# Graph network on one core: pair sums of the GAT passes made by TensorE and copied by ScalarE

## The reference

```python
def gatv2(x, src, dst, Wl, bl, Wr, br, att, bias, heads, out_ch):
    xl = (x @ Wl + bl).reshape(n, heads, out_ch)
    xr = (x @ Wr + br).reshape(n, heads, out_ch)
    e = jax.nn.leaky_relu(xl[src] + xr[dst], 0.2)
    score = jnp.einsum('ehc,hc->eh', e, att)
    smax = jax.ops.segment_max(score, dst, num_segments=n)
    ex = jnp.exp(score - smax[dst])
    denom = jax.ops.segment_sum(ex, dst, num_segments=n)
    alpha = ex / (denom[dst] + 1e-16)
    out = jax.ops.segment_sum(xl[src] * alpha[:, :, None], dst, num_segments=n)
```

## Time and profile before

| | |
|---|---|
| median of three runs | 7723.91 us |
| profiled execution, its own time | 7727.08 us |
| its span, first to last instruction | 7725.4 us |
| mean granted TensorE clock | 0.73 |
| busy: VectorE, GpSimd | 5362.1 us (69%), 4934.9 us (64%) |
| busy: TensorE products, weight loads | 4529.9 us (59%), 4074.4 us (53%) |
| busy: ScalarE | 870.3 us (11%) |
| first GAT pass, first gather to the pass's last add | 2569 to 3721 us |
| second GAT pass, likewise | 3782 to 4928 us |

### The profile page before, as it was taken

The page is one execution under the profiler, slowest core; times in us unless marked ns, Lnnn a source line. Parts: engine busy times, 40 slices in busy tenths (PEclk is TensorE's granted clock), DMA queues, the critical chain, the costliest instruction groups (busy, mean ns, idle before and its releaser), DMA issues. The chain is left out here.

```text
span 7725.4 us, 86513 instructions
## 1 busy us (share of the span) xinstructions
PE 4529.9 (59%) x24887; PEld 4074.4 (53%) x24887; DVE 5362.1 (69%) x14083; ACT 870.3 (11%) x2697; POOL 4934.9 (64%) x5168
## 2 busy tenths in 40 slices
PE   0444444566663466666466666675666677666665
PEld 0444343555553455555355555665555567555554
DVE  4333334577777799999799999647777744777776
ACT  0333332000000000000000000110000012000001
POOL 0777774777773577777377777227777702777771
PEclk8666666677776677777677777787777778777777
DMA  1444443666663344444344444456666635666662
GB/s 49 154 161 151 161 154 79 213 211 216 205 215 96 110 149 150 149 149 149 89 148 149 148 149 149 119 196 214 209 217 208 209 102 190 216 208 217 212 212 68
DMA packets 396869, 1264.58 MB, mean 164 GB/s; under 512 B 121860, under 2 KB 175678, under 8 KB 310014
## 3 DMA queue, kind: packets, MB, share of 16 engines
q1 hardware_dynamic: 195086, 766.00, 27.1%
q0 software_dynamic: 201328, 493.18, 22.5%
HBM read 1085.24 MB, written 173.47 MB: 163 GB/s over the span
## 5 line engine op out<-in xcount | busy, mean ns | idle before, releaser
L686 POOL DMA_INDIRECT gathered_rows<-table_l,gather_index x4176 | 4091.7, 980 | 1878.9 <-issue 1240.8
L1197 PE MATMUL ps<-weighted_rows,onehot 128*128 128x136 f32 (+2 forms) x8320 | 1744.9, 380 | 1508.4 <-DVE acc L1054 1507.1
L1197 PEld LDWEIGHTS ps<-weighted_rows,onehot 128*128 128x128 f32 x8320 | 1541.2, 274 | 1673.1 <-DVE acc L1054 914.7
L1164 PE MATMUL ps<-dst_side,onehot_t 128*128 x8320 | 1591.6, 353 | 140.3 <-issue 96.2
L1164 PEld LDWEIGHTS ps<-dst_side,onehot_t 128*128 128x128 f32 x8320 | 1456.3, 263 | 169.8 <-issue 98.7
L1054 DVE TENSOR_TENSOR acc<-acc,ps 128x136 f32 (+2 forms) x4160 | 1186.6, 285 | 108.6 <-PE ps L1197 7.6
L957 DVE TENSOR_TENSOR products<-gathered_rows,ps 128x512 f32<-128x512 f32 x836 | 565.1, 676 | 520.9 <-issue 227.9
L768 DVE TENSOR_TENSOR acc<-acc,ps 128x128 f32 x832 | 238.8, 287 | 693.7 <-PE ps L805 671.6
L977 DVE TENSOR_REDUCE scores<-products 128x16 f32<-128x512 f32 (+2 forms) x1040 | 709.4, 682 | 13.3
L686 POOL DMA_INDIRECT weights<-table_l,gather_index x612 | 579.6, 947 | 186.5 <-issue 172.8
L805 PE MATMUL ps<-gathered_rows,onehot 128*128 128x128 f32 x1664 | 351.5, 377 | 568.5 <-ACT gathered_rows L744 567.3
(11 more groups left out here) (283 smaller groups left out, 4450.9 us busy)
## 6 DMA issues: line engine op xcount, KB each, us to landing
onehot_t<-onehots_turned SPq DMA_DIRECT2D x260, 1024.0 KB
onehot<-onehots SPq DMA_DIRECT2D x260, 1024.0 KB, 5.2
gathered_rows<-table_l,gather_index POOLq DMA_INDIRECT x4176, 2.5
onehots<-onehot SPq DMA_DIRECT2D x52, 1024.0 KB, 6.9
onehots_turned<-onehot_t SPq DMA_DIRECT2D x52, 1024.0 KB, 4.2
table_l<-gathered_rows SPq DMA_DIRECT2D x50, 1024.0 KB, 4.4
segment_flags_sb<-segment_flags SPq DMA_DIRECT2D x1300, 8.2 KB
onehot<-type_mask_rows SPq DMA_DIRECT2D x50, 256.0 KB, 5.2
```

The lines of the kernel that those rows point to most:

```text
L686: pool.indirect_dma_start(out=home(v, t // GC)[:, t % GC, :], out_offset=None, in_=table, in_offset=bass.IndirectOffsetOnAxis(ap=e.idx[:, ...
L1164: ins = nc.tensor.matmul(ps[:, BZ + k, g * P:(g + 1) * P], e.ohT[:, u, t * P:(t + 1) * P], kRows[:, bass.ds(bs[t % 8], D)], start=True, st ...
L1197: ins = nc.tensor.matmul(ps[:, BP + n % 4, 256 * g:256 * g + PW], e.oh[:, u, t, :], exvT[:, t, :], start=True, stop=True)
```

## The change

In a GAT pass `dst_rows` on TensorE first multiplies the identity with the chunk's gathered rows, 512 columns in one product, and then accumulates the four destination products on it, so that the PSUM bank holds the pair sums. For that TensorE waits for the gathered rows. ScalarE copies the bank to `prod` (`keep_pair_sums`). VectorE's `product` is now the leaky step itself: the maximum of 0.2 times the bank and of the copy; `leaky` is gone. TensorE may write the bank again once that step is done, and ScalarE may write `prod` again once the score of two chunks earlier is done. Passes without `gat` are as before.

```diff
--- before.py
+++ after.py
@@ -907,6 +907,15 @@
                 e.oht_here[u].wait(act, a_no, 16 * (q + 1))
                 nc.scalar.activation(e.col0[:, u:u + 1], e.ohT[:, u, 0:1], ACT.Copy).then_inc(e.column_kept.sem, 1)
 
+            def keep_pair_sums(s, j):
+                if gat:
+                    c, k = J * s + j, j % 2
+                    e.z_ready.wait(act, a_no, c + 1)
+                    if not (static(s, 1) and j < 2):
+
+                        e.score_ready.wait(act, a_no, c - 1)
+                    nc.scalar.activation(e.prod[:, k, :], ps[:, BZ + k, :], ACT.Copy).then_inc(e.zc_ready.sem, 1)
+
             def keep_scores(s):
                 e.turned_ready.wait(act, a_no, s + 1)
                 if not static(s, 1):
@@ -933,11 +942,18 @@
                 if chain:
                     keep_scores(s - 1)
                 if cur:
+                    keep_pair_sums(s, 1)
                     keep_column(s, u, q)
+                    keep_pair_sums(s, 2)
                 if chain:
                     open_scale(s - 1, 1 - u)
                     exps(s - 1)
-
+                if cur:
+                    keep_pair_sums(s, 3)
+                    if ahead:
+                        keep_pair_sums(s + 1, 0)
+
+            keep_pair_sums(0, 0)
             for s in range(ways):
                 slot(s, s, 0, chain=s > 0, weigh=s > 1)
             turns(slot, ways, NG - 1, ways)
@@ -949,23 +965,22 @@
         def _(dve):
             def product(s, w, qw, j):
                 c, k = J * s + j, j % 2
+                if gat:
+                    e.zc_ready.wait(dve, gat_no, c + 1)
+                    V.scalar_tensor_tensor(e.prod[:, k, :], ps[:, BZ + k, :], 0.2, e.prod[:, k, :], ALU.mult, ALU.max)\
+                        .then_inc(e.prod_ready.sem, 1)
+                    return
                 v, qv = buffer(w, qw)
                 e.z_ready.wait(dve, a_no, c + 1)
                 here[v][j].wait(dve, here_no, 64 * (qv + 1))
                 if not (static(s, 1) and j < 2):
                     e.score_ready.wait(dve, a_no, c - 1)
                 V.tensor_tensor(e.prod[:, k, :].rearrange("p (g d) -> p g d", d=D), home(v, j)[:, :, 0:D],
-                                ps[:, BZ + k, :].rearrange("p (g d) -> p g d", d=D), ALU.add if gat else ALU.mult).then_inc(e.prod_ready.sem, 1)
-
-            def leaky(s, j):
+                                ps[:, BZ + k, :].rearrange("p (g d) -> p g d", d=D), ALU.mult).then_inc(e.prod_ready.sem, 1)
+
+            def weight_att(s, j):
                 if gat:
                     e.prod_ready.wait(dve, a_no, J * s + j + 1)
-                    pr = e.prod[:, j % 2, :]
-                    V.scalar_tensor_tensor(pr, pr, 0.2, pr, ALU.mult, ALU.max).then_inc(e.leaky_step.sem, 1)
-
-            def weight_att(s, j):
-                if gat:
-                    e.leaky_step.wait(dve, gat_no, J * s + j + 1)
                     pr = e.prod[:, j % 2, :].rearrange("p (g d) -> p g d", d=D)
                     V.tensor_tensor(pr, pr, att.unsqueeze(1).to_broadcast([P, GC, D]), ALU.mult).then_inc(e.att_step.sem, 1)
 
@@ -1093,8 +1108,6 @@
                     product(s, w, qw, 0)
                 if chain:
                     chain_backward(r, v)
-                if cur:
-                    leaky(s, 0)
                 if chain:
                     hand_back_ends(r)
                 if cur:
@@ -1111,8 +1124,6 @@
                 if weighs:
                     add(p, 3, bp[3])
                 if cur:
-                    leaky(s, 1)
-                if cur:
                     weight_att(s, 1)
                     score(s, 1)
                 if chain:
@@ -1126,7 +1137,6 @@
                 if weighs:
                     add(p, 5, bp[5])
                 if cur:
-                    leaky(s, 2)
                     weight_att(s, 2)
                 if weighs:
                     add(p, 6, bp[6])
@@ -1136,7 +1146,6 @@
                     add(p, 7, bp[7])
                 if cur:
                     product(s, w, qw, 3)
-                    leaky(s, 3)
                     weight_att(s, 3)
                     score(s, 3)
 
@@ -1155,14 +1164,20 @@
         def _(pe):
             def dst_rows(s, w, qw, j, bs):
                 u, q = two(w, qw)
+                v, qv = buffer(w, qw)
                 c, k = J * s + j, j % 2
+                if gat:
+                    here[v][j].wait(pe, here_no, 64 * (qv + 1))
                 if not (static(s, 1) and j < 2):
 
                     e.prod_ready.wait(pe, a_no, c - 1)
+                if gat:
+
+                    nc.tensor.matmul(ps[:, BZ + k, :], e.ident[:, :], home(v, j).rearrange("p g d -> p (g d)"), start=True, stop=False)
                 for g in range(GC):
                     t = GC * j + g
                     ins = nc.tensor.matmul(ps[:, BZ + k, g * P:(g + 1) * P], e.ohT[:, u, t * P:(t + 1) * P],
-                                           kRows[:, bass.ds(bs[t % 8], D)], start=True, stop=True)
+                                           kRows[:, bass.ds(bs[t % 8], D)], start=not gat, stop=not gat or g == GC - 1)
                 ins.then_inc(e.z_ready.sem, 1)
 
             def turn_scores(s):
```

## The result

| | before | after |
|---|---|---|
| four runs each: median (lowest to highest) | 7723.9 us (7718.52 to 7727.18) | 7667.86 us (7666.57 to 7673.8) |
| profiled execution, its span | 7727.08, 7725.4 us | 7667.10, 7665.4 us |
| VectorE busy | 5362.1 us | 5099.6 us |

The ratio is 0.9928, 95% interval 0.9912 to 0.9943.

The account below looks back on a forecast made before the run. VectorE set the GAT slot at 21.50 us, GpSimd close behind at 21.29. A new slot of 16.2 + 0.6 + 5.2 = 22.0 added 50 us over 100 slots, plus 5 for filling: 7780 us, range 7685 to 7930.

Parts of the forecast that it names:

- The chain's sum: GAT slot: VectorE's work, late TensorE sums, then the wait for weight columns behind chunk 0 and its copy; 22.0 us.
- The late sums: In a slot's VectorE work, TensorE's chunks 2 and 3 finish late for VectorE's adds, about 0.3 us each.
- T to A: From VectorE's slot start to the end of its first half's eighth add: 18.27 us before, 16.2 forecast without late sums.
- A to T: From the end of the first half's eighth add to VectorE's next slot start: 5.2 us, one slot in six 7.7.
- The higher clock around A: TensorE at 2.4 GHz around the first half's eighth add in most slots, since its 4.02 us pause ahead goes.
- no change: Rival: in the GAT passes the waits cancel, slot 21.4 us, kernel 7719 us, within 0.2% (15 us); chance 0.13.
- GpSimd's gathers and the port: GAT gathers are held by the attention product L970, which stays, so GpSimd keeps 21.29 us a slot.
- faster rival: In the GAT passes TensorE's clock rises and VectorE's saving comes through: 7709 or 7669 us; chance 0.22.
- second price: GAT gathers also get faster, so the chain's 20.9 us sets the slot: 55 us less, 7669; chance 0.18.
- The wait for gathered rows while the pipe fills: TensorE's new wait for gathered rows costs only at the start of the GAT passes: 5 us for both.
- The bound of 20.9: Lower bound in us of a GAT slot: 16.2 of VectorE work plus 4.7 at full clock; GpSimd then sets 21.29.
- the best of the faster rival: Fastest outcomes, with higher clock and VectorE's saving in the GAT passes; a tenth of chance left below 7685 us.

Follow-up runs that it names:

- two edits: Against the changed kernel: chunk 0's copy queued behind the weight columns, 7651.91 us; leaky step written to PSUM for the attention product, 7660.46; both, 7595.63.
- the experiment: Kernel before, with only the leaky step writing to the PSUM bank and the attention product reading it there: 7723.2 us, ratio 0.9996.

## Why the prediction was wrong

Two steps failed. The first made a loss of the forecast, the second put the result below the range.

- **The chain's sum: mis-sized.** "Slot: 16.2 + 0.6 + 5.2 = 22.0, against 21.5." The mechanism is there, the wait for the columns behind chunk 0 and its copy, but a full slot took 21.0 and 20.7. *The late sums:* 0.6 us a slot was added between T and A; T to A is 16.33 and 16.40 (medians) against 16.2, so it is 0.1 to 0.2. *A to T:* 5.2 was taken, the mean is 4.63 and 4.37. The higher clock around A came as argued, in about five slots of six, but the columns reach L1056 after 0.10 us, where 0.4 was taken from a row of a slot in which something else was last, and the slots at the lower clock took 5.7 to 6.0, not 7.7. Together this is 1.0 to 1.2 us of the 22.0, or 100 to 120 us. With it put right and GpSimd left at 21.29 the prediction's own sum gives 7709, no change by its own measure: 71 of the 112 us between forecast and result.
- **GpSimd's gathers and the port.** "So it is L970 that holds gathers up, and L970 stays. I leave GpSimd's 21.29 as it is". One gather that ended near L970's end, and one that ran free beside L964, were read as a pair. The second had started 0.02 us after L964 (3131.56 and 3131.54), the first 0.02 us ahead of it (3128.49 and 3128.51), too close to say from the starts which had its turn first. VectorE's lengths tell: of the 129 gathers of the pass that start within 0.05 us of an L964, 78 are held, and L964 takes 0.65 to 0.68 there; 51 run free, and L964 takes 0.70 to 0.76, as the 0.74 at 3131.54. Over all gathers it was L964, which the change removes in that form, beside which three quarters to four fifths of the excess stood (54.4 of 68.3 us, and 45.6 of 61.0 in the second pass). GpSimd's pace fell to 20.76 and 20.62; with 21.29 the kernel could have gained 15 us at most. This is the other 41 us.
- **The nearest rival was partly luck.** The faster rival's second price ("If the removed step L964 also held GpSimd") is 7669, within 2 us of the result, with a chance of 0.18. It names both mechanisms, but its sum took 4.7 us from A to T in every slot and no late sums; measured are 4.4 in most slots, 5.7 to 6.0 in one of seven and 0.1 to 0.2 of late sums, and these cancel.
- **The wait for gathered rows while the pipe fills:** 5 us were added, and about 1 us is seen. The first slot opening is not later (2618.5 against 2619.1), and one slot with such a wait is 1 us longer.
- **Right:** VectorE's removed work in T to A; the wait for the columns, 2.2 us a slot, 101 times; copy and columns back to back behind chunk 0 (but not the two copies: chunk 3's had ended 3.46 us earlier); the higher clock in the passes (0.84); the identity's product, 0.86 to 0.96 us from start to next start at the higher clock and 1.87 at the lower (3153.97 to 3155.84), against 0.86 and 1.72. VectorE's busy time fell by 262.5 us, not 286; its instructions overlap by some 0.07 us (one started at 3128.30 before, while that of 3127.70 ran to 3128.37), which busy time counts once. GpSimd did not begin to wait for the weighing, which was expected for slots of 22.0.
- **The bound of 20.9** for the chain was the right value, and the range was cut too close to it: "the best of the faster rival" was left out as a tenth, though each of its conditions had been argued for.

## What to carry to other kernels

Where two engines are within 1 or 2% of each other, price both for every removed instruction: a saving on one is worth nothing until the other has lost as much. Here two edits gave 16 and 7 us apart and 72 together. A cheap copy is placed by what stands behind it in its queue, not by its length. Which instruction holds a neighbour up is told by all its overlaps in the trace (where do the long ones end, which ran at their start), never by one or two rows.

## What the hardware showed

An indirect gather of 128 rows takes 0.94 us alone. One that starts while a VectorE instruction with two SBUF inputs runs ends 0.82 us after that instruction's end, so it takes up to 1.51 us beside one; the longest, 1.67, started 0.2 us ahead of L985, while L1021, a short instruction with two SBUF inputs, ran. Where both start within 0.05 us and the gather is not held, VectorE's instruction takes 0.70 to 0.76 instead of 0.65 to 0.68 us. Both inputs from one buffer (L964) count as two; with one of them in PSUM (L957, L971 of the experiment) no gather was held. The Trainium skill, SBUF — State Buffer, section "Who interferes with whom", says that a VectorE instruction with two SBUF inputs contends with a GpSimd instruction that reads SBUF, and these traces agree. The same section infers that `tensor_tensor` leaves descriptor generation alone. Here the gathers beside L985, a `tensor_tensor` with two SBUF inputs, lost 33.6 us, and those beside L964, a `scalar_tensor_tensor`, 54.4, so for indirect gathers the measurement decides against that.
